# A fused four-block layer on one core: the numerators of batch 0 in two PSUM banks, and new order lists for every pass

## The reference, cut to what matters

```
x = x + attn_a(layernorm(x))      # x: 16 batches x 512 tokens x 128
x = x + ffn(layernorm(x))         # top-2 of 8 experts and a shared one, 128 -> 512 -> 128
x = x + attn_b(layernorm(x))      # selective scan, 256 channels x 16 states
x = x + ffn(layernorm(x))

# attn_a: 16 heads of 8 dimensions, in each batch
q, k = elu(q) + 1, elu(k) + 1
attn_num   = einsum('bhid,bhjd->bhij', rope(q), rope(k))
attn_denom = einsum('bhid,bhjd->bhij', q, k)
out = einsum('bhij,bhjd->bhid', attn_num / attn_denom, v) @ w_out
```

## Time and profile before

| | |
|---|---|
| median of 3 runs | 3862.31 us (3858.8 to 3865.5) |
| the profiled execution | 3871.34 us, of it 3869.4 us from first to last instruction |
| busy | PE 3456.1 (89%), ACT 3236.8 (84%), DVE 2746.1 (71%), POOL 1277.1 (33%) |
| granted TensorE clock | 0.943 of full |
| FIRST pass | about 80 to 199 us of the span |
| SECOND pass | 199 to 419 us |
| passes 2 to 15 (MAIN) | 419 to 3525 us, 220 to 222 us each in the steady stretch |
| LAST and END | 3525 to 3869 us |

### The profile page before, as it was taken

The page is one execution under the profiler, slowest core; times in us unless marked ns, Lnnn a source line. Parts: engine busy times, 40 slices in busy tenths (PEclk is TensorE's granted clock), DMA queues, the critical chain, the costliest instruction groups (busy, mean ns, idle before and its releaser), DMA issues. The chain is left out here.

```text
span 3869.4 us, 38405 instructions
## 1 busy us (share of the span) xinstructions
PE 3456.1 (89%) x11446; PEld 1442.6 (37%) x11446; DVE 2746.1 (71%) x3513; ACT 3236.8 (84%) x4060; POOL 1277.1 (33%) x758
## 2 busy tenths in 40 slices
PE   3787699999999999999999999999999999998857
PEld 1131243434344343434444343434434343344424
DVE  2426667777686877878686777868687787868692
ACT  2667589998998989999998989999898999887663
POOL 1102243423233342423334242323334242314261
PEclk9586699999999999999999999999999999999978
DMA  4142336445354545436363644535454544534332
GB/s 147 46 136 61 117 123 184 143 148 160 121 174 131 176 138 178 152 122 195 116 185 123 179 148 140 168 122 175 142 169 133 185 145 134 179 99 160 122 127 101
DMA packets 214848, 552.02 MB, mean 143 GB/s; under 512 B 25105, under 2 KB 96626, under 8 KB 214642
## 3 DMA queue, kind: packets, MB, share of 16 engines
q1 hardware_dynamic: 214642, 549.57, 45.7%
HBM read 488.65 MB, written 63.18 MB: 143 GB/s over the span
## 5 line engine op out<-in xcount | busy, mean ns | idle before, releaser
L783 PE MATMUL bank<-hF,wst 128*128 128x512 f32 x2304 | 1171.9, 625 | 25.3 <-DVE tmp L1180 20.8
L1110 DVE TENSOR_TENSOR rPool<-bank,rPool 128x512 f32<-128x512 f32 x1024 | 703.1, 687 | 559.7 <-PE bank L713 514.1
L885 ACT ACTIVATE hF<-bank,cols 128x512 f32<-128x512 f32 x1152 | 770.9, 686 | 253.9 <-PE bank L774 245.5
L1330 POOL TENSOR_TENSOR yM<-yM,ws 128x1024 f32<-128x1024 f32 x240 | 595.1, 2479 | 1026.1 <-DVE ws L1229 1023.7
L1023 ACT ACT_TABLE_LOAD x554 | 710.8, 1283 | 9.7
L885 ACT ACTIVATE rPool<-bank 128x512 f32<-128x512 f32 x1024 | 571.2, 596 | 162.4 <-PE bank L708 156.9
L772 PE MATMUL bank<-xnH,wst 128*128 128x512 f32 x1152 | 599.5, 520 | 68.5 <-DMA wst<-wscr 36.4
L1222 DVE TENSOR_TENSOR_SCAN ws<-dAs,ws 128x1024 f32<-128x1024 f32 x256 | 635.5, 2487 | 6.9 <-ACT dAs L885 5.5
L1315 POOL TENSOR_TENSOR acc<-acc,tmp 128x512 f32<-128x512 f32 x240 | 353.1, 1471 | 835.7 <-DVE tmp L1180 827.3
L783 PEld LDWEIGHTS bank<-hF,wst 128*128 128x128 f32 x2304 | 412.7, 193 | 434.4 <-issue 347.7
L713 PE MATMUL bank<-qpk,kpk 48*128 48x512 bf16 x1024 | 420.3, 410 | 122.6 <-DVE rPool L1110 122.0
(11 more groups left out here) (157 smaller groups left out, 2948.4 us busy)
## 6 DMA issues: line engine op xcount, KB each, us to landing
wst<-wscr SPq DMA_DIRECT2D x288, 768.0 KB, 5.5
bc<-bcscr SPq DMA_DIRECT2D x256, 512.0 KB, 4.9
cB<-gscr SPq DMA_DIRECT2D x256, 256.0 KB, 4.8
qscr<-parts SPq DMA_DIRECT2D x192, 128.0 KB, 2.2
kscr<-parts SPq DMA_DIRECT2D x192, 128.0 KB, 3.7
kpk<-kscr SPq DMA_DIRECT2D x128, 192.0 KB, 6.0
qpk<-qscr SPq DMA_DIRECT2D x128, 192.0 KB, 6.5
wscr<-wst SPq DMA_DIRECT2D x9, 512.0 KB, 2.9
```

Source lines behind the costliest of these rows:

```text
L783: pe.matmul(ps[FFN][:, :], w2, hF[:, (NCH * f + q) % HSLOTS, :], start=(c == 0), stop=(c == FC - 1)).then_inc(s_dn, 1)
L885: return nc.scalar.activation(out_, in_, fn, **kw)
L1110: v.tensor_tensor(rP[:, slot, c, :], ps[NUM][:, :], rP[:, slot, c, :], ALU.mult).then_inc(s_mul, 1)
L1330: g.tensor_tensor(yM[:, :, :], yM[:, :, :], ws[:, s % 3, :, :], ALU.add).then_inc(s_ya, 1)
```

## The change

Two edits. The first gives the numerators of batch 0 two banks: even units stay in NUM, odd ones go to FFN, which no feed-forward uses until the SECOND pass. The wait of the numerator of unit n is then for the multiplication of n-2 instead of n-1, in batch 0 alone. The first `down` of all waits until the 64 multiplications of batch 0 are done, since it writes the same bank.

```diff
+        def num_bank(b, n):
+            return FFN if b == 0 and n % 2 else NUM
...
-                    pe.wait_ge(s_mul, floor(UNITS * b + n))
-                    pe.matmul(ps[NUM][:, :], lhs, rhs, start=True, stop=True).then_inc(s_num, 1)
+                    pe.wait_ge(s_mul, floor(UNITS * b + n - (b == 0)))
+                    pe.matmul(ps[num_bank(b, n)][:, :], lhs, rhs, start=True, stop=True).then_inc(s_num, 1)
...
+                    if q == 0 and f == 0:
+                        pe.wait_ge(s_mul, UNITS)
...
-                    v.tensor_tensor(rP[:, slot, c, :], ps[NUM][:, :], rP[:, slot, c, :], ALU.mult).then_inc(s_mul, 1)
+                    v.tensor_tensor(rP[:, slot, c, :], ps[num_bank(b, s)][:, :], rP[:, slot, c, :], ALU.mult).then_inc(s_mul, 1)
```

The second edit replaces the order lists of all engines in FIRST, SECOND, MAIN, LAST and END (and those of ACT and POOL in HEAD). The items are the same, but for the table loads: SECOND keeps 24, MAIN has 33 for 34, LAST 38 for 50. As an example, the list of SP in FIRST, and the end of SP's list in LAST:

```diff
-    P.in W.store*7 A.load*2 P.pk*4 P.ahead*2 W.store*2
+    P.in W.store*6 A.load W.store A.load W.store P.pk W.store P.pk*3 P.ahead*2
...
-    G.w*2 M.bc G.gate M.bc G.gate*2 M.bc*2 G.w G.gate M.bc*3 G.out
+    G.w M.bc G.gate G.w G.gate M.bc*4 G.gate M.bc*2 H.out G.out
```

More of the change, by code:

```diff
@@ L54 @@
     "ACT": """
-    P.load P.mean P.var P.qk*4 P.cast*8
+    P.load P.mean P.var P.qk*2 P.cast P.qk P.cast*2 P.qk P.cast*5
 """,
@@ L60 @@
     "POOL": """
-    P.keep P.rope P.rest*4 P.rope P.rest*4
+    P.rope P.rest*4 P.rope P.keep P.rest*4
 """,
@@ L72 @@
[L72 to L75, removed]
+    A.v A.den*6 P.load A.den A.num*2 A.den A.num A.den P.mean A.num A.av P.var A.den A.num*3 A.den*4 A.num*2 P.qk
@@ L85 @@
 """,
     "POOL": """
-    P.rope*2 P.rest*7 P.keep P.rest
+    P.rope P.rest P.rope P.rest*7 P.keep
 """,
@@ L91 @@
     "SP": """
-    F.w P.in F.w*3 F.rows F.gate*2 F.w*2 F.gate*2 F.w*2 F.gate F.w F.gate*3 A.load M.rows M.bc*2 A.load P.pk M.bc*5
-    P.pk*3 P.ahead*2
+    P.in F.w*3 F.rows F.gate F.w*2 F.gate*3 F.w F.gate F.w*3 F.gate*3 A.load M.rows M.bc*2 P.pk*2 A.load M.bc*2
+    P.pk*2 P.ahead M.bc*3 P.ahead
 """,
     "PE": """
-    A.v A.den*2 F.mean A.den A.num A.den*2 F.var A.den*2 F.router F.up*2 A.num F.up*2 A.num F.up F.down*2 A.den
-    A.num F.down A.av A.num A.den*2 F.turn F.down F.up A.num A.den P.load A.num F.down A.num A.den F.up*2 A.num A.av
@@ L98 @@
[L98 to L102, removed]
@@ L122 @@
+    M.hc*2 A.mul*5 M.dbx A.mul*2 M.dbx A.mul M.scan*2 M.hc*2 A.close
 """,
     "POOL": """
-    F.add*5 P.rope F.add*2 M.take P.rest*4 P.rope M.acc*3 M.keep M.acc P.rest*3 M.acc P.rest P.keep M.acc
+    F.add*4 P.rope F.add*3 M.take P.rest*3 P.rope P.rest*4 M.acc P.rest M.acc*5 M.keep P.keep
 """,
@@ L132 @@
+    M.bc G.w*2 M.bc*2 G.gate G.w P.pk G.w G.gate M.bc G.gate M.bc P.ahead*2 G.gate G.w
 """,
     "PE": """
-    A.v H.down*2 A.den*2 H.down A.den*2 H.down H.up*2 F.mean A.num A.den H.down*2 H.up*2 A.num H.up*4 F.var A.num
-    H.up H.down*2 A.den A.num A.den H.up A.av A.den*2 H.down*4 F.router A.num A.den*2 F.up*2 H.down*4 F.turn A.num
-    F.up*2 A.num A.den P.load H.close A.num A.den*2 P.mean F.down*3 A.num A.den P.var A.den A.num F.up A.av F.down
-    A.den*2 A.num F.up A.num F.up*5 F.down*4 P.qk A.den*2 A.num F.up A.num A.av A.num P.qk A.num A.den F.down*2
```

181 lines of the change are left out of this document (95 added, 86 removed).

## The result

| | before | after |
|---|---|---|
| median | 3862.97 us (3858.8 to 3865.5) | 3775.93 us (3763.91 to 3777.2) |
| the profiled execution, its span | 3871.34, 3869.4 | 3763.91, 3761.8 |
| granted TensorE clock | 0.943 | 0.963 |
| PE, ACT, DVE, POOL busy | 3456.1, 3236.8, 2746.1, 1277.1 | 3394.5, 3199.0, 2664.6, 1341.8 |

The account below looks back on a forecast made before the run. It took one-bank waits between PE and DVE to bound FIRST, late loads SECOND's start, PE and ACT MAIN, DVE's scans LAST. Gains of 25 + 12 + 28 + 3 = 68 us took the median from 3862.3 to 3794 (3748 to 3846).

Parts of the forecast that it names:

- Step 1: FIRST: two numerator banks shorten batch 0's attention from 119.7 to 95 us, a gain of 25 (10 to 41).
- circle over one bank: FIRST: numerator and DVE's multiplication wait for each other over one bank, 1.39 us a unit; two banks remove it.
- 79 us floor: FIRST: at the low clock PE's work totals 79 us, so batch 0's attention can't be shorter.
- rival B: FIRST: PE, less interrupted, regains full clock and ACT bounds FIRST at 85 us; 104 us in all, 3758; chance 14%.
- Step 2: SECOND's start: earlier casts of batch 1 remove the 12.88 us of idle PE; 12 us (6 to 15).
- pass 2's extra 11 us: Pass 2's time over a MAIN pass, left as it is like the rest of SECOND, 8 us either way.
- Step 3: MAIN, fourteen passes: the new order saves 2 us a pass, 28 us in all (0 to 56).
- changes of kind: MAIN: PE's list switches between kinds of matmul 229 times instead of 242, saving 1.8 us a pass.
- Step 4: LAST and END: twelve fewer ACT table loads, mostly hidden behind DVE's scans, gain 3 us (-5 to 12).
- A (batch 0 alone): Second bank and casts work, MAIN's new order only trades one wait for another: 37 us, 3825; chance 20%.
- C: MAIN: longer runs of up and down keep denominators from ACT; a pass grows 5 us, +30, 3892; chance 10%.
- D: FIRST: the second bank does nothing; casts and part of MAIN give 12 + 5 us, 3845; chance 6%.

Follow-up runs that it names:

- hybrid: Two banks with HEAD, FIRST, LAST and END lists of before, SECOND and MAIN lists of after: 3775.78 us, ratio 0.9791.
- old-LAST kernel: The changed kernel with the LAST and END lists of before on all engines: 3754.88 us, ratio 0.9724; a second time 3756.97 us, 0.9736.
- unpaired: The changed kernel with DVE's LAST list alone altered, scans one by one instead of two by two: 3779.23 us, ratio 0.9792.

## Why the prediction was right, and where it was wrong

| step | predicted | measured by the traces |
|---|---|---|
| 1. FIRST | 25 | 28.2 (22 to 28 in three traces of after) |
| 2. SECOND | 12 | 18.4 (18 to 21) |
| pass 2 | 2, its share of MAIN | 15.8 (16 to 19) |
| 3. MAIN, thirteen passes | 26 | 53.1 (44 to 54) |
| 4. LAST and END | 3 | -7.9 (-8 to -11) |

**Step 1** had the right time for a reason that was half right. The circle over one bank was real: with one bank the waits come back and FIRST ends at 209.0. From first logarithm to close the attention takes 94.3 us (95 predicted), and 98.7 and 100.3 in the other two traces of after. But the 79 us floor took the low clock for granted, and the clock came back in part, the premise of rival B. The bound then was nearer to ACT, which with the old order is busy 86% of the stretch. In after it is 80%, and 76 to 77% in the other two traces, at or below the 80 that I gave, since the new list of FIRST takes back what a better order has. The bank alone is worth 32.2 us there, and the new order, which I took for harmless, costs 4 to 13 of them.

One sentence of the Trainium skill, in "TensorE: Matmul & The Clock Gate", section "HAM oscillation — how this bites in real kernels", says that double-buffering in PSUM gave no further gain, of a matmul kernel whose loop had been reordered before. By it this term would have been 0. The bank alone gave 32 us, so it doesn't carry over to this kernel, where VectorE's multiplication stands between two matmuls of the same bank. In the same page of the Trainium skill the section "A second HAM failure mode: psum-queue depth-cycling" tells of a clock that goes back and forth while PE cycles through banks. The trace agrees in that: with two banks the clock falls and comes back four times in FIRST. But with one it stayed low for 88.7 us on end, so the mean rose from 0.66 to 0.86 all the same.

**Step 2** was right in mechanism and short in size. The early casts took the idle 12.88 us away. They also took away the low clock behind it, which the term left out; what is left of the 18.4 us for it is some 6. The hybrid, with late casts, shows both (217.8 us). The kernel with the old order of FIRST and early casts shows neither (199.6); besides the casts it differs up to there in the lists of HEAD and in those of SP and POOL in FIRST.

**The step that failed** is the clause "the rest of SECOND and pass 2's extra 11 us I leave as they are". Those 11 us were the same hole, 14.64 us of idle PE before the first denominator of pass 2, and they were in the trace. I had read the boundary FIRST to SECOND and not the next one. SECOND's new lists remove it; with SECOND's old lists pass 2 takes 235.3 again. Which of their moves does it wasn't tried.

**Step 3** was too low, and one of its two larger terms came to nothing. It priced 13 changes of kind fewer at 1.8 us of PE's time a pass and the waits at 3.2, and took 2 of the 5, as ACT would follow only in part. Measured are 4.1 (3.4 to 4.2). Eleven passes before and after (windows), a pass of before that had little low clock, then PE's waits in after:

```profile
872.00:3304.80 2432.80, 2307.01 (x7856) 968.14 (x7855) 1850.12 (x2366) 2207.38 (x2785) 851.47 (x517) 0.98 0.50 153
```

```profile
806.00:3192.10 2386.10, 2279.88 (x7864) 975.43 (x7864) 1799.02 (x2367) 2191.93 (x2775) 921.49 (x518) 0.99 0.51 156
```

```profile
1761.80:1980.00 218.20, 207.54 (x714) 87.36 (x712) 168.58 (x216) 199.89 (x253) 77.43 (x47) 0.99 0.49 154
```

```profile
PE bank L713 <- DVE rPool L1112: 38.2, 72, 1.0
PE bank L708 <- ACT rPool L887: 21.9, 44, 1.0
```

A pass is 4.2 us shorter: PE's busy time fell by 2.5 (27.1 / 11), its idle time by 1.8. The busy time looks like the term for the changes of kind, but it goes with the clock. In passes 3 to 15 the low clock stands for 99 us in before and 48 in after. From the first to the second trace of after it goes from 48 to 75, and PE's busy time goes up by 13.7 with the same program, half of the 27. At that rate the 51 us fewer are worth 26 of the 28.4 us by which PE's busy time fell in these thirteen passes (an estimate from the two traces). Those of the passes 3 to 14 that have the same 3.4 us of low clock say it directly. PE is busy 206.9 to 208.2 us in the five of them with the old list (before and bank alone), and 205.6 to 208.6 in the fifty with the new one, means 207.6 and 207.1; the pass of before shown above and the MAIN pass of after shown further up, with 206.6, are two of them. The whole pass takes 219.0 and 216.2 in the mean. So at an equal clock the new lists save 2.8 us a pass, nearly all of it idle time, and the rest of the 4.1 goes with less low clock. Why the clock is low less often in these passes wasn't tried.

The wait for `wst` fell from 16.6 to 1.4 us, that for numerators' banks from 49.7 to 38.2, and PE now waits 21.9 for logarithms, up from 9.0. ACT had room: it is busy 92% of the time, up from 91. Which of the lists' moves takes the idle time away wasn't separated.

**Step 4** had the wrong sign. The range of this term reached to -5. Fewer table loads (37 instead of 50 in the stretch) gave no gain on the whole. Two of DVE's waits between the last close and the end of LAST, in the third trace of after, and then in the old-LAST kernel of the same set:

```profile
DVE dte L1207 <- ACT ws L887: 14.5, 1, 14.5
DVE ws L1220 <- DMA bc<-bcscr: 11.5, 7, 3.0
```

```profile
DVE dte L1209 <- ACT ws L889: 1.4, 1, 1.4
DVE ws L1222 <- DMA bc<-bcscr: 1.0, 1, 1.0
```

Undoing the second was no gain. The first is one wait of 14.5 us for ACT in all seven traces with the new LAST lists, and of 1.4 us in all seven with the old ones. Against it the 25 scans after the last close take 60.5 to 61.6 us with the new lists (unpaired apart) and 78.4 to 79.1 with the old. So what DVE saves on scans, some 18 us, it gives back in these two waits (13 and 10), and more. That is bookkeeping and no experiment: a kernel that takes the 14.5 us away alone wasn't made, so the cause in LAST stays open. That these lists cost 6 to 11 us is shown.

**The rivals.** A (batch 0 alone) fell by the MAIN lists alone, 41 us. B's mechanism was right in part (the clock of FIRST came back to 0.86, not to 0.98), its time of 3758 18 us too low; its 85 us for the attention are nearly reached, with 86.2, by the old order with two banks and early casts. C would have needed a pass longer by 2.9 us; it got shorter by four. D fell by the one-bank run. The steps' errors (3, 6, 14, 27 and -11) add up to 40 us by the two profiled executions. Of these, 20 are the choice of executions: that of before lies 8 us above its median and that of after 12 below its own. By the medians the forecast is 18 us too high, and it would be 29 if LAST hadn't gone the other way: in part the errors cancelled, which is luck.

## What to carry to other kernels

When a boundary between two stages shows a hole, look at every later boundary of the same kind before pricing the change: here the same 13 to 15 us of idle PE stood at two, and at the first a stretch of low clock behind it cost some 6 us more. A second bank paid where another engine's work stood between two matmuls, and it is worth trying with the old order first: 32 us came from seven lines, and the best kernel of this study (0.9711) keeps most of FIRST's old order and all of LAST's. Judge a set of order lists pass by pass, compare busy times at an equal clock before calling them the order's work, and change one engine's list alone with care: SP's old one in MAIN cost 264 us, while an altered one of DVE in LAST cost nothing that is clear of the noise.
